# Vision transformer attention on one core: VectorE copies the turned row maxima in front of the third row maximum of its turn instead of behind it

## The chip, the cores and the metric

The kernel runs on one core of a Trainium2 chip. The metric is the device time of one execution in microseconds; lower is better. Engines are called by the names of the profile: PE is TensorE's matmul, PEld its weight load, DVE is VectorE, ACT is ScalarE, POOL is GpSimd, SP is SyncE, whose queue here issues nearly all DMAs.

## The reference, cut to what matters

The program is a vision transformer of four layers on 64 images, followed by text tokens, a small memory network and a mixture of experts. The change lies in the attention of the four layers:

```python
for i in range(DEPTH):                       # 4 layers, B = 64 images, NTOK = 197, 8 heads of 16
    y = layernorm(h, ln1_w[i], ln1_b[i])
    qkv = (y @ qkv_w[i] + qkv_b[i]).reshape(B, NTOK, 3, HEADS, hd)
    qkv = qkv.transpose(2, 0, 3, 1, 4)
    q, k, v = (qkv[0], qkv[1], qkv[2])
    attn = jax.nn.softmax(jnp.einsum('bhnd,bhmd->bhnm', q, k) * scale, axis=-1)
    o = jnp.einsum('bhnm,bhmd->bhnd', attn, v)
    o = o.transpose(0, 2, 1, 3).reshape(B, NTOK, DIM)
    h = h + (o @ proj_w[i] + proj_b[i])
    ...
```

## The kernel before, in words

All four layers lie in `layers_phase`. Images are taken in pairs, 32 pairs a layer, and one pass of the function `attn` of each engine is a **turn**: turn i works on pair i and prepares the pairs behind it. Every engine runs its own list of instructions; they meet through semaphores, and the order in which each engine takes its pieces is written out by hand in its `attn`. The middle of a layer (turns 4 to 23) is a hardware loop over four turns, the rest is written out. `live(k)` says that pair i + k exists; in a middle turn all pieces are there. Between two layers stand the turns of the MLP, in which only few attention pieces run.

q and k are held as three bf16 parts each (high, middle, low), stacked in the partitions of the tiles `q_st[p]` and `k_st[p]`. For each pair there are eight units u = 0..7 (two images, two halves of the heads, two halves of the tokens). A unit passes through the following.

1. PE `scores` (L351): four matmuls into the one tile `S`, 99 tokens by 4 x 197 scores. There is one `S` only, so the scores of unit u wait for the row maximum of unit u - 1 (semaphore `row_max`).
2. DVE `row_max` (L720): the negated maximum of each row of `S`, into `neg_max`. These two steps alternate through the whole turn: scores, maximum, scores, maximum. In turn i units 5 to 7 of pair i + 1 and units 0 to 4 of pair i + 2 pass through them.
3. When the eight maxima of pair i + 1 are there, POOL splits them into three bf16 parts (`max_parts`, L631 to L637), PE turns them by a matmul with the identity (L465, into `M2`, after the scores of unit 1 and the transposed scores of slot 4), and DVE copies the turned tile to SBUF as `max_rows` (L776 before the change; semaphore `max_copied`). SP then issues three small DMAs (L299, 32 pieces of 198 bytes each) that lay the three parts in the last rows of `q_st`, next to the queries.
4. PE `scores_t` (L368): the scores once more, transposed and with the maximum subtracted by the extra rows. The first unit of a pair waits until the three small DMAs have landed (semaphores `max_rd0`, `max_rd1`). ACT takes the exponential (L533), PE multiplies by v (L385), and so on to the projection.

PE works in eight slots a turn: slot j does one `scores` and one `scores_t`. The first slot of a turn has scores 5 of the next pair, then the first `scores_t` of its own pair. Slot 4 has scores 1, slot 5 scores 2, slot 6 scores 3, slot 7 scores 4. The turning matmul stands between slots 4 and 5, and in front of slot 6 stand two transposes (L407) and four matmuls for v (L476).

DVE's pieces around the change, in a middle turn: row maximum 0 and 1, `o_norm` (a reciprocal L728 and a multiplication L731, of the attention output of the pair before), row maximum 2, the copy, row maximum 3, four BN_AGGR, row maximum 4.

SP's order in a turn: wait for `max_copied`, three DMAs of the maxima (L299); then for each of the three parts of q and k, as POOL has them ready (L649, L653, L655), one write of q and one of k to DRAM (L307, 99 KB each, `spill_q` and `spill_k`); then wait until these six have landed, and load the stacks of a pair further on from DRAM (L314, three DMAs of k and three of q, 1.2 MB in all). All of these go through one hardware queue (q1), spread over 16 DMA engines.

```python
                    if then:
                        row_max(l, i + 2, p + 2, 1)
                    if last:
                        o_norm(l, i - 1, 1)
```

Of the kernel before, what the change touches and what calls it, by code (L numbers as in the profile page):

```python
# [40 lines left out]
def wait(eng, sem, value):  # L41

    if isinstance(value, int) and value <= 0:
        return
    eng.wait_ge(sem, value)


def wait_alone(eng, sem, value):

    if not isinstance(value, int):
        with eng.register() as count:
            eng.reg_mov(count, value)
            eng.wait_ge(sem, 1)
            eng.wait_ge(sem, count)
    else:
        wait(eng, sem, value)
# [127 lines left out]
def layers_phase(nc, g, A):  # L186

    with ExitStack() as ctx:
# [53 lines left out]
        def at(l, x):  # L242

            if isinstance(x, int):
                x = min(max(x, 0), PAIRS)
            return x + PAIRS * l
# [38 lines left out]
        with nc.Block() as block:  # L285
# [395 lines left out]
            def _(dve):  # L681
# [32 lines left out]
                def row_max(l, i, p, u):  # L714
                    b, half, c = u // 4, u // 2 % 2, u % 2
                    wait(dve, s["scores"], 8 * at(l, i) + u + 1)
                    if u == 0:
                        wait(dve, s["max_split"], 4 * (at(l, i) - 1))
                    out = neg_max[p % 2][:].rearrange("p (h b c) -> p h b c", b=2, c=2)[:, half * 4:half * 4 + 4, b, c]
                    nc.vector.tensor_reduce(out.rearrange("p (x y) -> p x y", x=2),  # L720
                                            S[0:TC, :, 0:2 * TB].rearrange("p x (y t) -> p x y t", y=2)[:, :, :, 0:NTOK],
                                            AX.X, ALU.max, negate=True).then_inc(s["row_max"], 1)

                def o_norm(l, i, b):
                    n = 2 * at(l, i) + b
                    wait(dve, s["o_turned"], n + 1)
                    o = M1[0:TC, :].rearrange("p (h e) -> p h e", e=32)
                    nc.vector.reciprocal(rec[:], o[:, :, HD]).then_inc(s["recip"], 1)  # L728
                    wait(dve, s["recip"], n + 1)
                    wait(dve, s["oT_turned"], n)  # L730
                    nc.vector.tensor_tensor(o_n[:].rearrange("p c (h e) -> p (c h) e", e=HD), o[:, :, 0:HD],  # L731
                                            rec[:].unsqueeze(2).to_broadcast([TC, 16, HD]),
                                            ALU.mult).then_inc(s["o_norm"], 1)

                def attn(l, i, p, even, live, y):
                    nxt, then, last = live(1), live(2), live(-1)

                    def bn(t0):
                        for t in (t0, t0 + 1):
                            op = nc.vector.bn_stats(stats[:, t, :], g.h[0:TC, bass.ds((i + 6) * 4 + t, 1), :]  # L740
                                                    .rearrange("p o d -> p (o d)"))
                        op.then_inc(s["stats"], 1)

                    if nxt:
                        row_max(l, i + 1, p + 1, 5)
                    if last:
                        o_norm(l, i - 1, 0)
                    if nxt:
                        row_max(l, i + 1, p + 1, 6)
                    if live(6):  # L750
                        wait(dve, s["aggr"], at(l, i + 6))
                        if isinstance(i, int):
                            wait(dve, s["m_h"], at(l - 1, i + 7))
                        bn(0)
                    if nxt:
                        row_max(l, i + 1, p + 1, 7)
                    if live(-2):
                        wait(dve, s["proj"], at(l, i - 1))
                        wait(dve, s["h_bias"], at(l, i - 1))
                        hp = g.h[0:TC, bass.ds((i - 2) * 4, 4), :]  # L760
                        nc.vector.tensor_tensor(hp, M0[0:TC, :].rearrange("p (t d) -> p t d", t=4), hp,
                                                ALU.add).then_inc(s["h_done"], 1)
                    if then:
                        row_max(l, i + 2, p + 2, 0)
                    if live(6):
                        bn(2)
                    if then:
                        row_max(l, i + 2, p + 2, 1)
                    if last:
                        o_norm(l, i - 1, 1)  # L770
                    if then:
                        row_max(l, i + 2, p + 2, 2)
                    if nxt:
                        wait(dve, s["max_turned"], at(l, i + 2))
                        wait(dve, max_rd[(p + 1) % 2], 48 * (even + (p + 1) // 2))
                        nc.vector.tensor_copy(max_rows[(p + 1) % 2][:], M2[0:96, 0:TC]).then_inc(s["max_copied"], 1)  # L776
                    if then:
                        row_max(l, i + 2, p + 2, 3)
                    if live(6):
                        wait_alone(dve, s["stats"], 2 * at(l, i + 6) + 2)  # L780
                        wait(dve, s["var_eps"], at(l, i + 6))
                        for t in range(4):
                            op = nc.vector.bn_aggr(mv[:, t, :], stats[:, t, :])
                        op.then_inc(s["aggr"], 1)
                    if then:
                        row_max(l, i + 2, p + 2, 4)

                def mlp(l, k, done):
# [22 lines left out]
                    if 0 <= k < PAIRS:  # L811
# [5 lines left out]
                                                ALU.add).then_inc(s["m_h"], 1)  # L817

                program(prep, attn, mlp)(dve)
        s.clear()  # L820

# [1201 lines left out]
```

## Time and profile before

| | us |
|---|---|
| runs of the kernel before | 4069.07, 4076.8, 4085.77 (median 4076.8) |
| the profiled execution, its own time | 4077.07 |
| its span, first to last instruction | 4075.3 |
| busy in the span: PE, DVE, POOL, ACT | 3523.8, 2503.2, 2284.3, 1907.3 |
| granted clock of PE, mean | 0.945 |

The profiled execution took 4077.07 us, of which 1.8 us lie outside its span, and it stands 0.3 us above the median of the runs. In a row of the trace the first two numbers are start and duration in us from the span's start; "[1.34 <-DMA x]" says that the engine was idle for 1.34 us before the instruction and that x released it. A row with "x4" merges four instructions in a row. A weight load (PEld) runs ahead of its matmul, so a wait shows on both, by about 0.2 us more on the load.

### The profile page before, as it was taken

The page shows a single profiled execution, that of the slowest core. Times are in us where ns is not written, and L with a number is a line of the kernel's source. Part 1 is how long each engine was busy: PE and PEld are TensorE (multiplying, and loading weights), DVE is VectorE, ACT ScalarE, POOL GpSimd, SP SyncE. Part 2 cuts the span into 40 slices and gives each one's busy share as a digit, 9 for nine tenths or more (in the row PEclk, how much of TensorE's full clock was granted, in tenths as well). Part 3 has the DMA queues.
Part 4 walks back from the last instruction along what each step waited for, and adds up shares of the span by engine and source line. Part 5 has one row for each costly group of instructions (what it writes and reads, how often), then busy time and mean ns, then how long its engine had stood idle before and what let it go on. Part 6 is the DMA issues. An engine that isn't in the chain of part 4 may idle for free. (4 is left out here: it accounts for less than half of the span.)

```text
span 4075.3 us, 91248 instructions
## 1 busy us (share of the span) xinstructions
PE 3523.8 (86%) x30780; PEld 2731.6 (67%) x30780; DVE 2503.2 (61%) x6419; ACT 1907.3 (47%) x3468; POOL 2284.3 (56%) x2633
## 2 busy tenths in 40 slices
PE   8779999888999888999987999988698887876983
PEld 8747777657777666777765777766344665655763
DVE  1246776546677555777654677755796887975110
ACT  0036666435666633666643666653464443322421
POOL 0056665465566366666446666625695663264876
PEclk9969999989999998999999999999898998998987
DMA  6556666025666314666502666620110223132432
GB/s 222 173 97 122 124 126 114 8 55 98 119 129 124 66 19 79 122 127 127 110 8 55 115 127 125 125 38 1 43 33 21 59 63 52 27 100 45 70 59 29
DMA packets 456050, 341.98 MB, mean 84 GB/s; under 512 B 70659, under 2 KB 440171, under 8 KB 455595
## 3 DMA queue, kind: packets, MB, share of 16 engines
q1 hardware_dynamic: 413635, 314.62, 37.5%
q0 software_dynamic: 27136, 16.42, 3.0%
q10 hardware_dynamic: 15008, 7.51, 0.7%
q8 instruction: 147, 2.41, 0.3%
q14 instruction: 124, 1.02, 0.1%
HBM read 227.69 MB, written 109.29 MB: 83 GB/s over the span
## 5 line engine op out<-in xcount | busy, mean ns | idle before, releaser
L720 DVE TENSOR_REDUCE a_neg_max<-a_S 99x4 f32<-99x788 f32 x1024 | 1003.5, 980 | 566.8 <-PE a_S L351 552.7
L533 ACT ACTIVATE a_probs<-a_St 99x792 f32<-99x792 f32 (+1 forms) x1024 | 851.2, 831 | 683.8 <-PE a_St L368 672.5
L368 PE MATMUL a_St<-a_q_st,a_k_st 99*99 99x198 bf16 (+1 forms) x4096 | 529.7, 252 | 90.5 <-DMA a_q_st<-a_max_rows 75.8
L351 PE MATMUL a_S<-a_k_st,a_q_st 96*99 96x197 bf16 x4096 | 552.1, 258 | 44.4 <-DVE a_neg_max L720 44.2
L351 PEld LDWEIGHTS a_S<-a_k_st,a_q_st 96*99 96x99 bf16 x4096 | 399.7, 128 | 266.5 <-DVE a_neg_max L720 220.4
L368 PEld LDWEIGHTS a_St<-a_q_st,a_k_st 99*99 99x99 bf16 (+1 forms) x4096 | 391.2, 126 | 122.5 <-DMA a_q_st<-a_max_rows 69.1
L385 PE MATMUL a_O<-a_probs,a_v_aug 99*32 99x198 f32 (+1 forms) x8192 | 466.4, 340 | 0.3
L663 POOL TENSOR_TENSOR h<-h,a_rows 99x512 f32<-99x512 f32 x128 | 162.8, 1272 | 275.1 <-DVE a_m_xn L801 275.1
L385 PEld LDWEIGHTS a_O<-a_probs,a_v_aug 99*32 99x32 f32 (+1 forms) x8192 | 247.0, 110 | 84.8 <-issue 2.1
L631 POOL CAST a_max_parts<-a_neg_max 99x32 bf16<-99x32 f32 x128 | 27.1, 212 | 471.1 <-DVE a_neg_max L720 471.1
L512 PEld LDWEIGHTS a_O<-a_w,a_gelu 128*99 128x99 f32 x2048 | 239.9, 167 | 45.0 <-issue 28.6
L816 DVE TENSOR_TENSOR h<-a_O,h 99x512 f32<-99x512 f32 x128 | 88.5, 692 | 289.2 <-PE a_O L512 289.2
L1746 POOL DMA_INDIRECT out<-h,token x128 | 211.4, 1651 | 95.0 <-DVE h L1796 39.5
L502 PE MATMUL a_St<-a_m_yT,a_w 128*128 128x396 f32 x512 | 213.2, 541 | 58.9 <-ACT a_m_yT L605 58.5
L649 POOL CAST a_parts<-a_q_k 128x792 bf16<-128x792 f32 x128 | 108.1, 844 | 273.9 <-issue 261.6
L512 PE MATMUL a_O<-a_w,a_gelu 128*99 128x128 f32 x2048 | 245.9, 273 | 3.5 <-DVE h L816 3.5
L599 ACT ACTIVATE a_gelu<-a_St,a_cols 128x396 f32<-128x396 f32 x256 | 150.9, 591 | 172.5 <-PE a_St L502 163.9
L651 POOL TENSOR_TENSOR a_q_k<-a_q_k,a_parts 128x792 f32<-128x792 f32 x128 | 216.5, 1692 | 10.3
L655 POOL TENSOR_TENSOR a_parts<-a_q_k,a_parts 128x792 bf16<-128x792 f32 x128 | 215.9, 1687 | 10.3
L160 PE MATMUL p_ps<-conv_w,xpatch 128*99 128x128 f32 x1536 | 170.6, 275 | 11.2 <-DMA xpatch<-in_x 11.2
L502 PEld LDWEIGHTS a_St<-a_m_yT,a_w 128*128 128x128 f32 x512 | 93.1, 199 | 127.7 <-ACT a_m_yT L605 80.8
L160 PEld LDWEIGHTS p_ps<-conv_w,xpatch 128*99 128x99 f32 x1536 | 170.4, 168 | 11.2 <-issue 11.2
(263 smaller groups left out, 7314.2 us busy)
## 6 DMA issues: line engine op xcount, KB each, us to landing
xpatch<-in_x SPq DMA_DIRECT2D x64, 594.0 KB, 3.7
spill_q<-a_parts SPq DMA_DIRECT2D x384, 99.0 KB
spill_k<-a_parts SPq DMA_DIRECT2D x384, 99.0 KB
a_k_st<-spill_k SPq DMA_DIRECT2D x128, 297.0 KB, 4.2
a_q_st<-spill_q SPq DMA_DIRECT2D x128, 297.0 KB, 6.4
a_k_st<-spill_k SPq DMA_DIRECT2D x128, 198.0 KB, 4.7
a_q_st<-spill_q SPq DMA_DIRECT2D x128, 198.0 KB, 6.7
a_k_st<-spill_k SPq DMA_DIRECT2D x128, 99.0 KB, 5.0
```

The lines of the kernel that those rows point to most:

```text
L160: mm = nc.tensor.matmul(ps[u][0:TC, c * D:(c + 1) * D], xb[:, u, k, c * TC:(c + 1) * TC], wc[:, k, :], start=(k == 0), stop=(k == KC - 1))
L351: mm = nc.tensor.matmul(S[0:TC, j // 2, j % 2 * TB:j % 2 * TB + NTOK], q_st[p % 4][0:SPLIT, head, b * TB + c * TC:b * TB + (c + 1) * TC], ...
L368: mm = nc.tensor.matmul(St[0:keys, j // 2, j % 2 * TB:(j % 2 + 1) * TB], k_st[p][:, head, first:first + keys], q_st[p][:, head, b * TB:(b ...
L385: mm = nc.tensor.matmul(O[32 * j:32 * j + 32, half * TB:(half + 1) * TB], v_aug[p % 4][0:keys, 2 * b + c, half * 4 + j, :], probs[0:keys, ...
L502: nc.tensor.matmul(St[:, h, 0:PW], m.w1[:, h * 128:(h + 1) * 128], m_yT[n % 2][:], start=True, stop=True).then_inc(s["m_fc1"], 1)
L512: mm = nc.tensor.matmul(O[0:TC, t * D:(t + 1) * D], gl[n % 2][:, h, t * TC:(t + 1) * TC], m.w2[:, h * D:(h + 1) * D], start=(h == 0), stop ...
L533: nc.scalar.activation(probs[0:keys, u % 4, :].rearrange("p (x t) -> p x t", x=2), St[0:keys, :, 0:2 * TB], ACT.Exp).then_inc(s["probs"], 1)
L651: nc.gpsimd.tensor_tensor(q_k[:], q_k[:], parts[:, 0, :, :], ALU.subtract).then_inc(s["res"], 1)
L655: nc.gpsimd.tensor_tensor(parts[:, 2, :, :], q_k[:], parts[:, 1, :, :], ALU.subtract).then_inc(s["lo"], 1)
L663: nc.gpsimd.tensor_tensor(hp, hp, m.b2.unsqueeze(1).to_broadcast([TC, 4, D]), ALU.add).then_inc(s["m_bias"], 1)
L720: nc.vector.tensor_reduce(out.rearrange("p (x y) -> p x y", x=2), S[0:TC, :, 0:2 * TB].rearrange("p x (y t) -> p x y t", y=2)[:, :, :, 0:N ...
L1746: nc.gpsimd.indirect_dma_start(out=out[:, :], out_offset=bass.IndirectOffsetOnAxis(g.token[0:n, e, k:k + 1].bitcast(U32), 0), in_=y[(2 * e ...
```

## The change

The three lines of the copy (two waits and the copy itself) go in front of the call for row maximum 2. Nothing else is changed; no other engine's list changes. In the kernel after the change the copy is L774.

```diff
                     if last:
                         o_norm(l, i - 1, 1)
-                    if then:
-                        row_max(l, i + 2, p + 2, 2)
                     if nxt:
                         wait(dve, s["max_turned"], at(l, i + 2))
                         wait(dve, max_rd[(p + 1) % 2], 48 * (even + (p + 1) // 2))
                         nc.vector.tensor_copy(max_rows[(p + 1) % 2][:], M2[0:96, 0:TC]).then_inc(s["max_copied"], 1)
+                    if then:
+                        row_max(l, i + 2, p + 2, 2)
                     if then:
                         row_max(l, i + 2, p + 2, 3)
```

DVE, a turn in the hardware loop, from the normalisation of the attention output to row maximum 3 (L45 and ISA rows are the register work and waits of the loop; - is before, + is the change):

```order
 L728 RECIPROCAL a_rec<-a_M 99x16 [waits o_turned]
 L731 TENSOR_TENSOR a_o_n<-a_M,a_rec 99x256 [waits oT_turned,recip]
-L45 REGISTER_ALU
-L720 TENSOR_REDUCE a_neg_max<-a_S 99x4 [waits scores]
 L45 ISA [waits max_turned]
-L776 CAST a_max_rows<-a_M 96x99 [waits max_rd1]
+L774 CAST a_max_rows<-a_M 96x99 [waits max_rd1]
+L45 REGISTER_ALU
+L720 TENSOR_REDUCE a_neg_max<-a_S 99x4 [waits scores]
 L45 REGISTER_ALU
 L720 TENSOR_REDUCE a_neg_max<-a_S 99x4 [waits scores]
```

The copy now follows the multiplication L731 directly, and row maximum 2 comes behind the copy, right in front of row maximum 3.

DVE, the last turn ahead of the first pair of a layer, which has no `o_norm`; from row maximum 0 to the BN_AGGR:

```order
 L720 TENSOR_REDUCE a_neg_max<-a_S 99x4 [waits scores] x2
 L740 BN_STATS a_stats<-h 99x6 x2
-L720 TENSOR_REDUCE a_neg_max<-a_S 99x4 [waits scores] x2
-L776 CAST a_max_rows<-a_M 96x99 [waits max_turned]
-L720 TENSOR_REDUCE a_neg_max<-a_S 99x4 [waits scores]
+L720 TENSOR_REDUCE a_neg_max<-a_S 99x4 [waits scores]
+L774 CAST a_max_rows<-a_M 96x99 [waits max_turned]
+L720 TENSOR_REDUCE a_neg_max<-a_S 99x4 [waits scores] x2
 L783 BN_AGGR a_mv<-a_stats 99x2 [waits var_eps,stats]
 L783 BN_AGGR a_mv<-a_stats 99x2 x3
```

Here the copy comes between row maxima 1 and 2.

## Rows read from the trace of the kernel before

**Rows 1.** The page's costliest groups: transposed scores, matmuls and weight loads.
```profile
L368 PE MATMUL a_St<-a_q_st,a_k_st 99*99 99x198 bf16 (+1 forms) x4096 | 529.7, 252 | 90.5 <-DMA a_q_st<-a_max_rows 75.8
...
L368 PEld LDWEIGHTS a_St<-a_q_st,a_k_st 99*99 99x99 bf16 (+1 forms) x4096 | 391.2, 126 | 122.5 <-DMA a_q_st<-a_max_rows 69.1
```

**Rows 2.** The copy's tile: its instructions, and who waited for it (us, times).
```profile
L776 DVE CAST a_max_rows<-a_M x128: 248/249/260, 262.9 to 2702.8; 96x99 bf16<-96x99 f32 x128
...
  PE a_St L368: 75.8, 72
```

**Rows 3.** Timeline of DVE, the copies alone: five turns in a row.
```profile
405.66 0.25 DVE L776 CAST a_max_rows<-a_M 96x99 bf16<-96x99 f32 x1
...
419.68 0.25 DVE L776 CAST a_max_rows<-a_M 96x99 bf16<-96x99 f32 x1
...
435.03 0.25 DVE L776 CAST a_max_rows<-a_M 96x99 bf16<-96x99 f32 x1
...
449.05 0.25 DVE L776 CAST a_max_rows<-a_M 96x99 bf16<-96x99 f32 x1
...
464.55 0.25 DVE L776 CAST a_max_rows<-a_M 96x99 bf16<-96x99 f32 x1
```

**Rows 4.** Timeline of all engines around the copy at 435.03.
```profile
432.59 0.21 PE L465 MATMUL a_M<-a_ident,a_max_parts 99*96 99x99 bf16 x1
...
433.56 0.54 PE L351 MATMUL a_S<-a_k_st,a_q_st 96*99 96x197 bf16 x4
...
433.63 0.42 DVE L731 TENSOR_TENSOR a_o_n<-a_M,a_rec 99x256 f32<-99x256 f32 x1
...
434.14 0.98 DVE L720 TENSOR_REDUCE a_neg_max<-a_S 99x4 f32<-99x788 f32 x1
...
434.45 1.04 PE L476 MATMUL a_M<-a_w,a_yT 128*99 128x128 f32 x8
...
435.22 0.41 PEld L351 LDWEIGHTS a_S<-a_k_st,a_q_st 96*99 96x99 bf16 x4
```

**Rows 5.** Timeline: SP's DMA issues of two turns, and POOL's last part.
```profile
415.93 1.44 SPq L314 DMA_DIRECT2D a_q_st<-spill_q  x3
419.95 1.83 SPq L299 DMA_DIRECT2D a_q_st<-a_max_rows  x3
...
422.55 1.69 POOL L655 TENSOR_TENSOR a_parts<-a_q_k,a_parts 128x792 bf16<-128x792 f32 x1
...
424.48 0.56 SPq L307 DMA_DIRECT2D spill_q<-a_parts  x1
...
429.70 1.44 SPq L314 DMA_DIRECT2D a_q_st<-spill_q  x3
435.31 1.84 SPq L299 DMA_DIRECT2D a_q_st<-a_max_rows  x3
```

**Rows 6.** Timeline: the first transposed scores behind the copies at 419.68 and 435.03.
```profile
425.04 0.34 PEld L368 LDWEIGHTS a_St<-a_q_st,a_k_st 99*99 99x99 bf16 x4 [1.34 <-DMA a_q_st<-a_max_rows]
...
439.02 0.38 PEld L368 LDWEIGHTS a_St<-a_q_st,a_k_st 99*99 99x99 bf16 x4
```

**Rows 7.** DMA issues from 413 to 418 us, the last load: KB, us to landing.
```profile
a_q_st<-spill_q SPq DMA_DIRECT2D x1, 99.0 KB, 6.9
```

**Rows 8.** DMA packets from 422.5 to 423.0, then from 437.0 to 437.5 us.
```profile
DMA packets 127, 0.02 MB, mean 47 GB/s; under 512 B 115, under 2 KB 127, under 8 KB 127
...
DMA packets 48, 0.01 MB, mean 13 GB/s; under 512 B 48, under 2 KB 48, under 8 KB 48
```

**Rows 9.** Two more copies; between them a wait and a window (busy us, then granted clock).
```profile
357.96 0.25 DVE L776 CAST a_max_rows<-a_M 96x99 bf16<-96x99 f32 x1
...
363.94 0.34 PEld L368 LDWEIGHTS a_St<-a_q_st,a_k_st 99*99 99x99 bf16 x4 [1.96 <-DMA a_q_st<-a_max_rows]
...
366.00:368.00 2.00, 2.00 (x13) 2.00 (x12) 1.37 (x3) 0.91 (x2) 0.00 (x0) 0.50 0.07 17
...
375.54 0.25 DVE L776 CAST a_max_rows<-a_M 96x99 bf16<-96x99 f32 x1
```

## The prediction

> **What bounds the kernel now.** I read the page's costliest groups first. The transposed scores wait 90.5 us on PE in all, 75.8 of them for the three small DMAs that carry the turned maxima, and 69.1 us on the weight loads, which see the same waits [rows 1]. That is the only DMA that PE waits for in attention, and it is what an earlier copy could bring forward. The view of the copy's tile says that there are 128 copies, 32 a layer, and that PE waited 72 times for their DMAs [rows 2].
>
> Next comes the length of a turn, from one copy to the next. In the timeline of DVE the four turns from 405.66 to 464.55 take 14.02, 15.35, 14.02 and 15.50 us [rows 3]. The reader is to see the alternation. Long and short turns take turns, and two in a row make 29.37 and 29.52 us. So the pair of turns is the steady quantity, and I ask first what fixes it.
>
> The first transposed scores say which turn is long: after the copy at 419.68 the weight load starts at 425.04, held for 1.34 us by the small DMA. After the copy at 435.03 it starts at 439.02 and is held by no DMA [rows 6]. Both copies are followed by the same issue, 0.27 us later and 1.83 us long [rows 5]. So the same issue lands after 5.3 us the one time and in under 4.0 us the other.
>
> The difference is what stands in front of it in the one hardware queue. SP issued the q stack of a later pair from 415.93 to 417.37, 2.3 us ahead of the copy at 419.68, and from 429.70 to 431.14, 3.9 us ahead of the copy at 435.03 [rows 5]. The last load of the three, issued at about 416.9, lands 6.9 us later, at 423.8 [rows 7]. The DMA packets agree: from 422.5 to 423.0 us 115 of 127 packets are small (under 512 B), right when the loads run out, and at 437.0 there is nothing else on the engines but small ones, 48 in half a microsecond [rows 8]. In the long turn the maxima stand behind 1.2 MB of stacks. They land at 425.0, 1.2 us after the last load.
>
> This explains the alternation. The loads go out at a fixed distance behind the copy of the turn before (419.68 to 429.70: 10.0 us), since they wait for the parts of q and k to be written. A long turn gives them more time ahead of the next maxima, which then wait for nothing. A short one gives less, and the next turn waits. In numbers: a turn is 14.02 us of work or as long as the loads hold it, whichever is more, and the sum of two is held at 29.37 by the loads.
>
> **The change part by part.**
>
> *The copy comes earlier.* It now starts behind L731, which ends at 434.05, so at about 434.1 instead of 435.03: 0.93 us earlier [rows 4]. Its own wait costs nothing. The turning matmul ended at 432.80 [rows 4], and in PE's list it stands ahead of scores 2, so DVE cannot be held by it longer than by the scores that it would wait for anyway. `max_rd` waits for DMAs two turns old.
>
> *Row maximum 2 comes later.* It starts at 434.14 now, just when both of its conditions are met: L731 is done at 434.05 and scores 2 end at 434.10 [rows 4]. The copy of 0.25 us goes exactly there. The next instruction can start some 0.1 us before the end of the one in front (the copy at 435.03 starts 0.09 us before the maximum ends, 434.14 + 0.98 = 435.12). So the delay is 0.12 us at least, and at most 0.3 us, if the copy starts at 434.14 and lasts to its end with a gap. I take **0.2 us**. Is anything behind it idle? The next weight load of the scores starts at 435.22, 0.10 us after the maximum, while the v matmuls still run until 435.49 [rows 4], so PE hides almost nothing and the turn's work becomes 14.02 + 0.2 = 14.22 us.
>
> *What of this shows.* In a turn that waits for the DMA the 0.2 us come off the wait, since the landing does not move. In a turn that does not wait they lengthen it, and the loads then have 0.2 us more ahead of the next maxima. Either way the sum of two turns stays 29.37 as long as 2 x 14.22 = 28.44 is less. So the 0.2 us are covered in the middle of the layers. If that cover were gone, they would cost 108 x 0.2 = 21.6 us. Not covered are the turns with little DMA in them, about five a layer at its two ends: 20 x 0.2 = **+4.0 us**.
>
> *What the earlier DMA brings.* Bounds for the landing in a turn with a wait: nothing, if the maxima only stand in the queue longer, and 0.93 us, if they were late by their own issue. The nearest row is the one at 422.5: the small packets already follow the loads without a gap, so there is no hole that an earlier issue would fill. That is close to the lower end. I take 0.1 us, for turns in which the third small DMA just comes too late. Page "DMA: Bandwidth & Descriptors" of the Trainium skill (Queues, rings and completion order) speaks against the change: on one DMA engine a semaphore increment lands only after every earlier write of that engine. By it this 0.1 us would be 0 and the sum 5.4 us worse. The trace agrees with the rule in the two turns of rows 6.
>
> *What the earlier issue does to SP's list.* The writes of the high part now go out about 0.9 us earlier. They gain nothing by themselves, because the loads wait for the low part: POOL ends it at 424.24 (422.55 + 1.69) and SP issues its write at 424.48 [rows 5]. At most 0.24 us can be won. The issues of the middle part end only just before 424.48, so I take 0.05 us.
>
> Together 0.15 us a pair of turns. Of the 128 turns 108 are in the middle, 54 pairs: 54 x 0.15 = **-8.1 us**.
>
> *The clock.* In the turn from 357.96 to 375.54 (17.58 us) the weight load waits 1.96 us for the small DMAs, and from 366 to 368 us PE has a granted clock of 0.50 [rows 9], the lower of its two levels, 1.2 GHz. It fell after PE had stood idle for the DMA. The turn is 3.56 us above 14.02, and 1.96 of it is the wait: the other 1.6 us are the slow clock's. The timeline of the copies has nine such turns of 17 us and more beside the first of each layer. With 0.2 us taken off every wait, and the landing a little earlier, I let three of the nine fall out, at 1.6 us each: **-4.8 us**.
>
> Sum: 4077.1 + 4.0 - 8.1 - 4.8 = **4068 us**. The profiled execution lies 0.3 us above the median of the runs, so the same number holds for the median.
>
> **The rivals.**
>
> *The maxima are late by their own issue.* Then the landing moves by the whole 0.93 us. For it: the wait is put down to their DMA, and the copy does stand 0.9 us later than it must. Against it: one and the same issue lands under 4.0 us and at 5.3 us after the copy [rows 5, 6]. The pair of turns would fall from 29.37 to 28.44, which is also its new floor of work: -54 x 0.93 + 4.0 = -46.2, 4031 us; a few more slow-clock turns saved give 4026. The Trainium skill, page "DMA: Bandwidth & Descriptors" (Anatomy of one DMA), gives a DMA a fixed cost of about 2 us whatever its size, by which this rival would be right. Rows 6 do not bear that out in the long turn.
>
> *The tail behind the loads shrinks.* The 1.2 us between the last load and the last of the maxima are partly issue: three DMAs 0.6 us apart. If early queueing halves them, the pair falls by 0.5: -27 + 4 - 5, 4049 us. For it: the third small DMA is issued at 421.2, close to the end of the loads. Against it: the small packets run on seamlessly at 422.5 [rows 8].
>
> *The delay is not covered, and the kernel is slower.* The place is row maximum 2 in front of slot 6. The price is 0.2 us in each of 108 middle turns and 4.0 at the ends, nothing gained: 4077 + 21.6 + 4.0 = 4103 us, and 4114 with 0.3 us. It decides if the loads move back with the turn, that is, if their time is counted from row maximum 2 and not from the q and k of the turn. For it: PE has next to no slack at 435.22 [rows 4], and every maximum gates the next scores. Against it: the low part is done by POOL from q and k that were made before this point, and the turns without a wait are all 14.02 us, 0.67 us under the mean of 14.69, which is room for three such delays.
>
> **How the numbers follow.** Forecast 0.72, issue-bound 0.11, shorter tail 0.08, uncovered delay 0.09. A measurement of this kernel can tell about 0.5% (20 us) from no change: faster means under 4056, slower over 4097. Faster takes the second and third case, 0.18 with the edge of my own (own range 4053 to 4084: the delay from 0.12 to 0.3, the landing from 0 to 0.3, the clock from 0 to -15). Slower is the fourth, less its milder half: 0.07. Same is the rest, 0.75. The range reaches down to 4045, for the shorter tail, and up to 4087, for a delay that is covered only in part. It leaves out the issue-bound case and most of the uncovered one, about 0.2.
>
> **What would show it.** The copy directly behind L731, ahead of row maximum 2; row maximum 2 starting 0.1 to 0.3 us later than scores 2 allow; turns without a DMA wait at 14.1 to 14.3 us instead of 14.02; and, the main step, two turns in a row still at 29.2 to 29.4 us, with waits for the small DMAs shorter by about the delay. The total wait of PE for them should fall from 75.8 to between 45 and 65 us, and this is mostly delay that took its place. The prediction is wrong if the pair falls to 28.5 us with the waits nearly gone (issue-bound), or if turns of 14.2 us are followed by the old waits of 1.1 us in full (uncovered).

## The result, and the profile after

The changed kernel takes 4027.43 us (median of 6 runs, 4016.06 to 4032.91) against 4074.57 us for the kernel before (6 runs, 4062.84 to 4085.77). The ratio is 0.9883, with a 95% interval of 0.9861 to 0.9904. A repeat later, on another chip, gave 0.9856 (0.9827 to 0.9885). The change is 1.2% faster, five times what was forecast, and the time lies below the forecast range. The profiled execution took 4032.91 us, 44 us less than the profiled execution of the kernel before.

| | before | after |
|---|---|---|
| median of 6 runs, us | 4074.57 | 4027.43 |
| profiled execution, us | 4077.07 | 4032.91 |
| PE waits for the maxima's DMAs, us (times) | 75.8 (72) | 33.0 (53) |
| mean granted clock | 0.945 | 0.945 |

The page's costliest groups of the changed kernel answer to [rows 1]:

```profile
L368 PE MATMUL a_St<-a_q_st,a_k_st 99*99 99x198 bf16 (+1 forms) x4096 | 526.9, 251 | 47.4 <-DMA a_q_st<-a_max_rows 33.0
...
L368 PEld LDWEIGHTS a_St<-a_q_st,a_k_st 99*99 99x99 bf16 (+1 forms) x4096 | 389.0, 126 | 77.9 <-DMA a_q_st<-a_max_rows 38.5
```

The waits fall by 42.8 us on PE. I had forecast a fall of 11 to 31 us, most of it with VectorE's delay in its place. The profiled time fell by 44 us, no less than the waits did, so no other wait took their place. How the 44 us are made up is worked out further down.

Timeline of all engines of the changed kernel, the same place as [rows 4] (start us, us, engine):

```profile
435.94 0.54 PE L351 MATMUL a_S<-a_k_st,a_q_st 96*99 96x197 bf16 x4
...
436.00 0.42 DVE L731 TENSOR_TENSOR a_o_n<-a_M,a_rec 99x256 f32<-99x256 f32 x1
...
436.35 0.25 DVE L774 CAST a_max_rows<-a_M 96x99 bf16<-96x99 f32 x1
436.52 0.98 DVE L720 TENSOR_REDUCE a_neg_max<-a_S 99x4 f32<-99x788 f32 x1
```

The copy starts at 436.35, 0.07 us before L731 ends (436.42), and row maximum 2 starts at 436.52, 0.17 us after the copy starts. Scores 2 end at 436.48. In [rows 4] row maximum 2 starts 0.04 us after the scores end, and here also 0.04 us. The distance is 0.04 us in all 128 turns of the kernel before and in 127 of the changed one (0.10 us in the one left). **The copy delays row maximum 2 by nothing.**

Timeline of SP and POOL for the same turn, and the next copy; it answers to [rows 5]:

```profile
436.62 1.84 SPq L299 DMA_DIRECT2D a_q_st<-a_max_rows  x3
438.59 0.64 SPq L307 DMA_DIRECT2D spill_q<-a_parts  x1
...
440.23 0.56 SPq L307 DMA_DIRECT2D spill_q<-a_parts  x1
...
440.29 1.69 POOL L655 TENSOR_TENSOR a_parts<-a_q_k,a_parts 128x792 bf16<-128x792 f32 x1
...
442.00 0.57 SPq L307 DMA_DIRECT2D spill_q<-a_parts  x1
442.61 0.57 SPq L307 DMA_DIRECT2D spill_k<-a_parts  x1
445.56 1.33 SPq L314 DMA_DIRECT2D a_k_st<-spill_k  x3
...
450.57 0.25 DVE L774 CAST a_max_rows<-a_M 96x99 bf16<-96x99 f32 x1
```

Read these from row maximum 2 (436.52), which I take as the zero of the turn in both kernels, since it follows its scores by the same 0.04 us in both. POOL ends the low part at 441.98, and SP issues its write 0.02 us later. The last write is issued by 443.18, 6.66 us after row maximum 2, and the loads begin at 445.56, 9.04 us after it. In the kernel before, the same two events stand 6.9 and 9.8 us after row maximum 2 (medians). The loads of the stacks begin 0.7 us earlier. The experiments test whether this, and not the earlier issue of the maxima, is where the gain comes from.

To compare kernels I worked out, from the timeline of each trace, the medians over the 96 turns of pairs 4 to 27 of each layer, all counted in us from the start of row maximum 2. "Tail" is from the last landing of the loads in front to the last landing of the maxima. "Two turns" is the length of two turns in a row, also called the pair below. The two rows come from one profiled execution each. The repeat of the change, profiled on another chip, has 28.81 us for two turns and 1.07 us for the tail, so differences of 0.1 us in these two columns are not to be read as effects.

| kernel | maxima issued | last write issued | loads begin | tail | two turns | turns of 17 us and more |
|---|---|---|---|---|---|---|
| before | 1.17 to 3.01 | 6.88 | 9.77 | 1.09 | 29.38 | 6 |
| after | 0.11 to 1.94 | 6.66 | 9.06 | 1.03 | 28.69 | 1 |

### The profile page after: what moved, and what is told of

It is laid out like the page before. It is cut to its first block and busy times, and to the rows that moved or that the text cites. A ratio compares the mean times of both kernels' runs of the same rounds, so it can differ in the third digit from the quotient of the medians.

```text
span 4031.1 us, 91248 instructions
## 1 busy us (share of the span) xinstructions
PE 3521.2 (87%) x30780; PEld 2730.6 (68%) x30780; DVE 2494.7 (62%) x6419; ACT 1907.3 (47%) x3468; POOL 2286.2 (57%) x2633
## 3 DMA queue, kind: packets, MB, share of 16 engines
q14 instruction: 124, 1.02, 0.1%
```

## The experiments

Theory A: the gain comes over SP's list. The writes go out earlier, so the loads begin earlier, and the maxima stand behind them for less long. Theory B: the maxima land earlier because they are issued earlier. Theory C: the new order on VectorE is worth something by itself.

### The maxima early, the writes late

```diff
+                            if part == 0 and live(0):
+                                wait_alone(sp, s["probs"], 8 * at(l, i) + 7)
                             for qk in range(2):
```

> The changed kernel, but SP issues the writes of the high part of q and k only once the exponential of unit 6 of the turn is done, which is about where they went out in the kernel before. The maxima stay early. Theory A (the gain comes over SP's list: the writes go out earlier, so the stacks are loaded earlier, so the maxima stand behind them for less long): the gain is lost, 4065 to 4080 us, two turns in a row at 29.2 to 29.5 us. Theory B (the maxima land earlier because they are issued earlier): the gain stays, 4025 to 4035 us, two turns at 28.7 us.

This kernel, the next two and the first of the kernels with one small DMA ran beside the kernel before at 4079.65 us. Measured: 4052.01 us, ratio 0.9948 (0.9922 to 0.9974), two turns at 29.09 us. More than half of the gain is gone, though the maxima go out exactly as early as in the change. Against B, which had 4025 to 4035; A's own number was missed as well. The reason is in SP's timeline of this kernel, in a turn whose row maximum 2 starts at 437.06:

```profile
437.17 1.85 SPq L299 DMA_DIRECT2D a_q_st<-a_max_rows  x3
440.03 0.64 SPq L309 DMA_DIRECT2D spill_q<-a_parts  x1
...
443.22 0.57 SPq L309 DMA_DIRECT2D spill_k<-a_parts  x1
446.49 1.32 SPq L316 DMA_DIRECT2D a_k_st<-spill_k  x3
```

The writes are six in a row again, but they start 2.97 us after row maximum 2, not 3.12, and the loads begin after 9.43 us (median 9.49), not 9.77. The hold was a little too short to restore the old start of the loads.

### Maxima and writes late, VectorE in the new order

```diff
                         wait(sp, s["max_copied"], at(l, i + 2))
+                        if live(2):
+                            wait(sp, s["row_max"], 8 * at(l, i + 2) + 3)
```

> The changed kernel, but SP waits for row maximum 2 before it issues the small DMAs, so SP's list runs at the times of the kernel before, while VectorE keeps its new order. Theories A and B both: no gain left, 4065 to 4080 us. Theory C (the new order on VectorE is worth something by itself, by work taken out from between row maxima 2 and 3): 4025 to 4040 us. If the copy in front of row maximum 2 costs VectorE 0.2 us, the turns without a wait are 14.2 us; if nothing, 14.02.

Measured: 4057.71 us, ratio 0.9947 (0.9922 to 0.9973), two turns at 29.04 us, the shortest turns at the old 14.02. C expected 4025 to 4040 us and is out: the gain does not come from the order on VectorE. A and B both expected 4065 to 4080 us and were missed too: here too the loads begin a little too early, after 9.48 us, since SP no longer waits for the copy behind row maximum 2 (the first of the maxima is issued 1.01 us after its start, against 1.17 before the change).

```profile
432.25 1.88 SPq L301 DMA_DIRECT2D a_q_st<-a_max_rows  x3
434.26 0.65 SPq L309 DMA_DIRECT2D spill_q<-a_parts  x1
...
437.46 0.57 SPq L309 DMA_DIRECT2D spill_k<-a_parts  x1
440.65 1.32 SPq L316 DMA_DIRECT2D a_k_st<-spill_k  x3
```

(Row maximum 2 of this turn starts at 431.25, so the loads begin 9.40 us after it.) **These two kernels together decide between A and B.** The last of the maxima is issued by 1.94 us in the first and by 2.84 us in the second, 0.9 us apart. The loads begin at 9.49 and 9.48 us, and two turns take 29.09 and 29.04 us. Issuing the maxima 0.9 us earlier is worth nothing that these traces can tell, which is to about 0.1 us a pair.

### The loads late, nothing else changed

```diff
                         wait(sp, s["scores_t"], 8 * at(l, i + 1))
+                        if not isinstance(i, int):
+                            wait(sp, s["row_max"], 8 * at(l, i + 2) + 8)
```

> The changed kernel, but in the 80 looped turns SP issues the stack loads only after row maximum 7 of the next turn, about 0.5 us later than it does now, and later still when the turn itself waits. Nothing of the maxima is changed. Theory A: the loads now move back with the turn, so each looped turn waits about 0.9 us and takes about 14.9 us, the alternation disappears, 4060 to 4085 us. Theory B: no difference, 4025 to 4035 us.

The hold stands only in the 80 turns of the hardware loop. Measured: 4065.61 us, ratio 0.9952 (0.9927 to 0.9976). In its profiled execution (4078.39 us) the median turn is 14.90 us, as A has it, and of the 96 turns only 9 are shorter than 14.06 us, where the change has 32. B expected no difference to the change, 4025 to 4035 us, and is out. The maxima are issued at the change's 0.11 to 1.94 us, and PE waits for them for 74.9 us, as long as before the change:

```profile
  PE a_St L370: 74.9, 94
```

One thing does not fit the medians: this kernel is 0.3 to 0.5% faster than the kernel before (the medians, 4065.61 and 4079.65 us, give 0.9966), though its median pair is the longer one (29.91 against 29.38 us). Two facts account for a part. Its profiled execution was the slowest of its six (4056.01 to 4078.39 us), and it had three turns of 17 us and more where the kernel before had six. The sum of the 96 turns is only 6.7 us above that of the kernel before. So for this kernel the median pair gives the direction against the change, but not its time against the kernel before; why is open.

### One small DMA instead of three, in either order

```diff
-                        for part in range(3):
-                            sp.dma_start(q_st[(p + 1) % 4][SPLIT + part:SPLIT + part + 1, :, :]
-                                         .rearrange("o h (x t) -> o (h x) t", t=TC),
-                                         max_rows[(p + 1) % 2][part * 32:(part + 1) * 32, :]).then_inc(max_rd[(p + 1) % 2], 16)
+                        sp.dma_start(q_st[(p + 1) % 4][SPLIT:SPLIT + 3, :, :].rearrange("r h (x t) -> r (h x) t", t=TC),
+                                     max_rows[(p + 1) % 2][:]).then_inc(max_rd[(p + 1) % 2], 16)
```

The two waits on `max_rd` count 16 a turn instead of 48. First in the old order on VectorE, then in the new one:

> The kernel before with its order on VectorE, but the three small DMAs of the maxima are one DMA of 96 pieces, so SP's list is 1.2 us shorter per turn. Theory A: the low part is again issued as soon as POOL has it (the writes are as early as in the change), and the tail behind the loads shrinks from 1.1 us to 0.5 us: two turns at 28.0 to 28.3 us, 4000 to 4020 us. Theory B: the one DMA is issued at the time of the first of the three, so it lands about 1.2 us earlier than the last of them: 4010 to 4030 us, and most of what is left is still there to be gained by an earlier copy.

> The changed kernel with one small DMA in place of three. Theory A (SP's list and the queue): in the old order of VectorE the one DMA already let the low part go out as soon as POOL has it, so the earlier copy adds nothing any more: within 6 us of the kernel with one DMA in the old order, loads first issued 9.06 us after row maximum 2 starts, two turns at 28.4 to 28.6 us. Theory B (the issue time of the maxima counts): another 15 to 30 us faster than that kernel, since the one DMA goes out 1.07 us earlier still.

Measured, old order: 4006.31 us, ratio 0.9832 (0.9791 to 0.9872); new order, on another chip: 4025.83 us, ratio 0.9838 (0.9806 to 0.9870). The kernel before took 4079.65 us beside the first and 4092.82 us beside the second, so the ratios are to be compared, and they are the same. With the issue of the maxima 1.1 us shorter the old order already begins its loads at 9.06 us, the change's time, and an earlier copy then adds nothing. That is A. B expected the new order to be another 15 to 30 us faster. The sum of the 96 turns differs by 1.6 us (1376.3 and 1374.7 us). A was wrong on the size: the tail fell only from 1.09 to 0.86 us, not to 0.5, and two turns take 28.60 us in the old order, not 28.0 to 28.3. In the new order they take 28.63 us, where A had 28.4 to 28.6. Beside the change itself (0.9856 on the same chip as the new order) the one DMA is worth perhaps 0.2%, within the intervals.

The repeat of the change, which that chip ran beside them:

> The changed kernel as it is, beside the others on the same chip. All theories: 1.0 to 1.4% faster than the kernel before.

It took 4036.25 us, the kernel before 4092.82.

### The small DMA on a queue of its own

```diff
                         nc.scalar.activation(q_k[:, 0, :], M0[:, 0:PW], ACT.Identity, bias=m.bq).then_inc(s["q_f"], 1)
+                    if live(1):
+                        wait(act, s["max_copied"], at(l, i + 2))
+                        nc.scalar.dma_start(q_st[(p + 1) % 4][SPLIT:SPLIT + 3, :, :].rearrange("r h (x t) -> r (h x) t", t=TC),
+                                            max_rows[(p + 1) % 2][:]).then_inc(max_rd[(p + 1) % 2], 16)
```

SP's own DMA of the maxima is taken out, and the waits on `max_rd` count 16 a turn as above.

> As the one before, but ScalarE issues the one small DMA on its own queue, in front of the exponential of unit 5, so it does not stand behind the stack loads in SP's queue. Theory A, if the order is kept within a queue only: the wait for the maxima disappears, nearly all turns take 14.02 us, and the time falls to 3975 to 3995 us, unless the issue on ScalarE delays the exponentials (then 14.1 to 14.3 us a turn). Theory A2 (the order holds on each DMA engine across its queues, as far as the semaphore's increment goes): the maxima still land only once the loads in front of them on their engine have, and the time stays within 10 us of the kernel with one small DMA on SP. Theory B: no difference to that kernel either, since the issue time is the same.

Measured: 4052.11 us, ratio 0.9894 (0.9864 to 0.9924), slower than the same DMA on SP (0.9838, beside it on the same chip). The DMA lands no earlier from its own queue: the tail is 0.82 us, against 0.84 us with one queue, and from the end of the issue to the last landing it is 4.0 us, against 4.2 us. A's 3975 to 3995 us is out. A2 had the landing right; its time (within 10 us of the kernel with one small DMA on SP) was missed by the price of the issue, below. DMA packets of this kernel from 457.0 to 458.0 us, by queue (q10 is ScalarE's):

```profile
q1 hardware_dynamic: 235, 0.17, 88.7%
q10 hardware_dynamic: 55, 0.01, 9.8%
```

The DMA was issued from 455.12 to 455.87. The first of its 99 packets starts at 457.39 and the last ends at 458.61, beside the last packets of SP's loads. In the eight turns of this kernel (pairs 30 and 31 of each layer) in which SP's queue moves nothing large meanwhile, the same DMA lands 2.6 us after the end of its issue. The one small DMA on SP's queue takes 2.65 us in such turns, so the 4.0 and 4.2 us both hold about 1.4 to 1.5 us that come with the loads, whichever queue the DMA is on. Both queues run on the same 16 DMA engines, which is the likely reason; what held the packets there was not taken apart. The issue also has a price on ScalarE. Timeline of the same turn:

```profile
455.12 0.75 ACTq L573 DMA_DIRECT2D a_q_st<-a_max_rows  x1
...
456.04 0.83 ACT L527 ACTIVATE a_probs<-a_St 98x792 f32<-98x792 f32 x1 [0.98 <-PE a_St L362]
...
456.92 0.34 PEld L362 LDWEIGHTS a_St<-a_q_st,a_k_st 99*99 99x99 bf16 x4 [0.43 <-ACT a_probs L527]
```

The exponential of unit 5 starts at 456.04, behind an issue that ends at 455.87, while the scores that it reads had ended by 455.32. PE's weight load waits 0.43 us for it. The median turn becomes 14.43 us. I had expected 14.1 to 14.3.

### k first: the loads begin earlier still

If A is right, any earlier start of the loads must shorten the pair, whatever is done with the maxima. So here nothing of the maxima is touched. Each part's k is written ahead of its q, and the k stacks are loaded once the three writes of k have landed.

```diff
-                            for qk in range(2):
+                            for qk in (1, 0):
...
-                                             parts[:, part, qk, :]).then_inc(part_wr[p % 2], 16)
-                        wait_alone(sp, part_wr[p % 2], 96 * (even + p // 2 + 3))
+                                             parts[:, part, qk, :]).then_inc((part_wr, part_wk)[qk][p % 2], 16)
+                        wait_alone(sp, part_wk[p % 2], 48 * (even + p // 2 + 3))
...
                         for qk, st in ((1, k_st[p]), (0, q_st[p])):
+                            if qk == 0:
+                                wait_alone(sp, part_wr[p % 2], 48 * (even + p // 2 + 3))
```

(POOL's wait on `part_wr` becomes one on each of the two.)

> The changed kernel, with each part's write of k issued ahead of that of q, and the k stacks loaded as soon as the three writes of k have landed (own semaphores for k and q). Nothing of the maxima or of the order on VectorE differs from the change. Theory A: the loads begin about 0.6 us earlier (8.4 to 8.5 us after row maximum 2 starts, against 9.06), the pair of turns would fall from 28.6 by 0.6 to 0.75, so it reaches the 28.04 of pure work: most turns 14.02 to 14.1 us, 96 turns x 0.3 = 25 to 30 us faster than the change, ratio to the kernel before 0.978 to 0.981. Theory B (the issue time of the maxima counts): no difference to the change, ratio 0.985 to 0.988.

> The same on the changed kernel with one small DMA in place of three. Theory A: the tail behind the loads is 0.2 us shorter still, so practically no turn waits: 14.02 us in nearly every one, ratio to the kernel before 0.975 to 0.980. Theory B: as the kernel with one small DMA, ratio 0.983 to 0.984.

Measured: 4010.26 us, ratio 0.9796 (0.9751 to 0.9841), and with one small DMA 3992.27 us, ratio 0.9755 (0.9710 to 0.9801). A had 0.978 to 0.981 and 0.975 to 0.980, B 0.985 to 0.988 and 0.983 to 0.984: both are as A has them, and the second is the fastest of all. SP's timeline of the first, one turn whose copy starts at 430.53:

```profile
430.81 1.84 SPq L300 DMA_DIRECT2D a_q_st<-a_max_rows  x3
...
436.19 0.56 SPq L308 DMA_DIRECT2D spill_k<-a_parts  x1
436.80 0.56 SPq L308 DMA_DIRECT2D spill_q<-a_parts  x1
438.88 1.32 SPq L317 DMA_DIRECT2D a_k_st<-spill_k  x3
440.37 1.32 SPq L317 DMA_DIRECT2D a_q_st<-spill_q  x3
```

The last write is issued by 437.36, and the loads begin 1.5 us later; in the turn of the change shown above it was 2.4 us. Timeline of DVE in the same kernel, its copies:

```profile
430.53 0.25 DVE L778 CAST a_max_rows<-a_M 96x99 bf16<-96x99 f32 x1
...
444.55 0.25 DVE L778 CAST a_max_rows<-a_M 96x99 bf16<-96x99 f32 x1
...
458.57 0.25 DVE L778 CAST a_max_rows<-a_M 96x99 bf16<-96x99 f32 x1
...
472.59 0.25 DVE L778 CAST a_max_rows<-a_M 96x99 bf16<-96x99 f32 x1
```

Three turns in a row take 14.02 us, where [rows 3] has 14.02 and 15.35 in turn. PE's waits for the maxima are 11.2 us in 14 places, and with one small DMA 5.3 us in 7:

```profile
  PE a_St L371: 11.2, 14
```

All kernels together, medians over the same 96 turns:

| kernel | maxima issued by | loads begin | tail | two turns | turns under 14.06 us |
|---|---|---|---|---|---|
| loads late | 1.94 | 10.41 | 1.05 | 29.91 | 9 |
| before | 3.01 | 9.77 | 1.09 | 29.38 | 35 |
| writes late | 1.94 | 9.49 | 1.04 | 29.09 | 16 |
| maxima and writes late | 2.84 | 9.48 | 1.02 | 29.04 | 31 |
| after | 1.94 | 9.06 | 1.03 | 28.69 | 32 |
| the change, repeated | 1.95 | 9.05 | 1.07 | 28.81 | 34 |
| one small DMA, old order | 1.95 | 9.06 | 0.86 | 28.60 | 33 |
| one small DMA, new order | 0.88 | 9.07 | 0.84 | 28.63 | 37 |
| one small DMA on ScalarE's queue | 0.85 | 9.05 | 0.82 | 28.86 | 4 |
| k first | 1.94 | 8.34 | 1.04 | 28.05 | 72 |
| k first, one small DMA | 0.89 | 8.39 | 0.86 | 28.04 | 79 |

From before to after the loads begin 0.71 us earlier and the pair is 0.69 us shorter; the two holds lie on the same line (0.29 and 0.34). The pair stops at 28.04, twice 14.02. The column of the maxima follows no such line: 1.94 us stands beside 29.91, 29.09, 28.69 and 28.05. The DMA on ScalarE's queue stands off the line because its turns are held by the exponential and not by the loads.

## Why the prediction was wrong, point by point

**What bounds the kernel: right.** The maxima stand behind the loads, a turn is 14.02 us or what the loads make it, and the sum of two is held. The tail did not move with the issue of the maxima (1.02 to 1.09 us over an issue time that moved by 1.1 us). The 0.1 us taken for it was small enough: 0.06 us in the change, 0.02 us in its repeat. The rule quoted from page "DMA: Bandwidth & Descriptors" of the Trainium skill (Queues, rings and completion order), by which an increment lands only after every earlier write of its engine, would have given 0, and these traces agree to 0.06 us. The Trainium skill's page says "across its queues"; a queue of its own left the tail at 0.82 us, which agrees too, though here the packets themselves had waited, so it is no test of the increments alone.

**"What the earlier issue does to SP's list": this step failed.** It gave 0.05 us for the earlier start of the loads, and measured it is 0.71 us a pair. It has two halves.

- The issue of the low part. I bounded it by 0.24 us and took 0.05, because the issues of the middle part ended only just before 424.48. But they ended there because SP issued all its writes back to back behind the late maxima, and the same 0.9 us moves them too. In the median the last write is issued by 6.66 us in place of 6.88: 0.22 us, nearly the whole bound.
- The landing of the writes. I said that the writes of the high part "gain nothing by themselves". With six writes issued in a row the loads began 2.8 us after the last issue. With gaps between the parts they begin 2.4 us after it. That is 0.42 us (medians 2.82 and 2.40), which I had nowhere in the sum. The two kernels with late writes bunch them again and have 2.74 and 2.72. It is the landing that moves: the last write lands 2.73 us after its issue before the change and 2.25 us after it in the change. That the gaps go with the faster landing is read from these four kernels; the cause on the DMA engines was not taken apart.

54 pairs x 0.71 us are 38 us where the text has 2.7. That is the main term of the miss.

**"Row maximum 2 comes later": 0.2 us forecast, 0.00 measured.** I took the copy to begin when L731 had ended and the next instruction 0.1 us before the copy's end. In fact it starts 0.07 us before L731 ends and holds VectorE for 0.17 us, just until the scores arrive. So the shortest turns stay at 14.02 us, and since row maximum 2 is as close behind its scores at the ends of the layers as in the middle, the +4.0 us there are absent too. My lower bound (0.12) was too high, since it allowed the overlap on one side of the copy only.

**The clock: right in kind, too small.** Of the 96 turns six took 17 us and more before the change, and one after. At the forecast's 1.6 us each that is about 8 us, against -4.8 us. In these 96 turns the granted clock was at its lower level for 23.9 us before and for 6.8 us after. Over the whole program it was there for 449 and 443 us, so the mean stays at 0.945. The repeat has two such turns; these are single executions. (The forecast's nine turns outside the first of each layer are eight in the trace.)

Together: the sum of these 96 turns fell by 44.0 us (1427.9 to 1383.9 us), the rest of the program by 0.2 us. 48 pairs x 0.69 us = 33 us, and the slow clock's estimate of 8 us, leave 3 us open. Counted by waits it closes about: PE's waits for the maxima in these turns fell by 36.0 us (59.5 to 23.5 us), and with the 8 us that makes 44.

**The rivals.** "Late by their own issue" gave 4031 us and so was nearest to the time, with the wrong mechanism: it is refuted by the holds and by k first. Its own tests speak against it as well: the pair fell to 28.69 and not to 28.44, and PE still waits 33 us. A right number was no evidence here. The section that this rival quotes from the Trainium skill (page "DMA: Bandwidth & Descriptors", Anatomy of one DMA) describes the path of DMAs that GpSimd issues. The maxima go through a hardware queue. On that queue the third small DMA landed 1.5 us after the end of its issue when the queue was empty, and 3.1 us after it in the other turns of the change. The uncovered delay did not exist. The shorter tail did not come with the change. Two sums there are slightly off: with 0.3 us of delay the uncovered case comes to 4116 us and not 4114, since the ends take 6.0 us then, and the lower ends of the own range add up to 4046 us and not 4053. Neither changes the forecast.

## What to carry to other kernels

When an engine's list issues DMAs in order, moving one of them earlier can move all that is issued behind it, until something else holds them. Here the first write moved by 1.1 us, the last by 0.2 us and the loads by 0.7 us. Follow each of these to the transfer that the critical wait stands behind, down to the landing and not only to the issue. In this queue, held by 1.2 MB of loads, what counted for the small DMAs was when the loads in front of them began, not when they were issued themselves. When a turn and the next one share a sum, test a theory with a second edit that moves the same quantity by other means: loading k ahead of q was worth 0.6 to 0.9% on top, and was found from the line between the start of the loads and the pair.

## What the runs showed of the hardware

- On VectorE the copy started 0.07 to 0.08 us before the end of the multiplication in front of it, and row maximum 2 as much before the copy's end: the 0.25 us copy held the engine for 0.17 us.
- The last of six writes was followed by the start of the loads after 2.40 us when the six were spread over 4.6 us (the change), and after 2.82 us when they were issued within 3.8 us (the kernel before).
- A small DMA on ScalarE's queue did not pass the loads on SP's queue: 4.0 us from the end of its issue to its landing, as on SP (4.2 us), and 2.6 us where there were no loads. Its issue, 0.74 us, held ScalarE.
